# Three images' queries and the last context's high parts move into the end of the linear attention, and the high parts get two buffers

## Chip, cores and metric

The kernel runs on one core of one Trainium2 chip. The time is the device time of one launch in microseconds (us), the median of several runs. The profile is of one further execution.

## What is computed

The program is two layers of a network on x, 4 images of 512 tokens with 256 channels, each sublayer followed by a residual and a layer norm. Only layer 1's linear attention and its cross attention are touched by the change. The context `y` has 1601 tokens of 192 channels for each image.

```python
def _L1_attn_ref(H, W_qkv, b_qkv, W_proj, b_proj, gamma, beta):
    qkv = jnp.einsum('bnd,ed->bne', H, W_qkv) + b_qkv
    q, k, v = ...                            # 16 heads of 16
    q = _phi(q)                              # elu(x) + 1
    k = _phi(k)
    kv = jnp.einsum('bhnd,bhnv->bhdv', k, v)
    ...
    out = qkv_out / jnp.clip(qk1, 1e-06, None)
    out = out.reshape(B, N, D)
    out = jnp.einsum('bnd,ed->bne', out, W_proj) + b_proj
    out = (out - mu) * jax.lax.rsqrt(var + LN_EPS) * gamma + beta
    return out + residual

def _L1_xattn_ref(x, y, Wq, bq, Wk, bk, Wv, bv, Wo, bo):
    q = x @ Wq + bq
    k = y @ Wk + bk
    v = y @ Wv + bv
    ...                                      # 8 heads of 32
    weight = jnp.einsum('bhqd,bhkd->bhqk', q, k) * scale
    weight = jax.nn.softmax(weight, axis=-1)
    out = jnp.einsum('bhqk,bhkd->bhqd', weight, v)
    return out @ Wo + bo

x = _layernorm(x + _L1_attn_ref(x, ...), axis=-1)
x = _layernorm(x + _L1_xattn_ref(x, ctx_768, ...), axis=-1)
```

## The kernel before

The stages run one after the other, and a stage ends when all five engines have waited for its last results (`settle`). Within a stage each engine's program is written by walking one list of steps, the plan. An engine takes its instructions strictly in that order and waits on semaphores for what others deliver, so the plan sets the order of work on TensorE (PE), VectorE (DVE), ScalarE (ACT), GpSimd (POOL) and in SP's DMA queue alike.

**Linear attention** (`linear_plan`). For each image b: `inputs` (the projections to q, k and v), `state`, `read`, `regroup` (transposes, 16 stores to DRAM and one load back, `la_rg`), `project` (output projection, then a norm chain on DVE of evictions, statistics, scaling and the gamma multiply L2016, with the beta sum on POOL), `close` (residual L2020 and the second norm) and `channels` (transposes of the result into `x_ch`). With these, `mingle` spreads a side list evenly: work of the cross attention that doesn't depend on x, for images 0 to 2 (`AHEAD` is 3).

**The side list.** Matrix products of float32 data are made of bfloat16 parts, a high part and the rest (low). For the context of an image, `parts` is two casts on ACT (`xa_c_high` L2162 and `xa_c_both` L2163), and `context` is the subtraction of `xa_c_low` on DVE (L2134) and one on POOL in `xa_c_both` (L2178). `keys` (4 steps for an image, L2110, with ACT L2170 and DVE L2139 behind them) and `value` (7 steps, L2120, DVE L2145) read these parts. `keys`, and `value`, use the PSUM pairs of banks 0 and 2 in turn. There is one buffer of each part, so that `parts` of image b+1 waits for the last `value` of image b.

**Cross attention** (`cross_plan`). A prefix comes first: for each of the 4 images `x_split` (ACT casts `x_ch` into the high half of `xa_x_hl` L2554, POOL subtracts the low half L2623), two `queries` steps of 6 matmuls (L2369; ACT L2564 writes the high half, DVE L2474 the low half of `xa_q_hl`) and `asked` (SP stores it to DRAM, L2334); image 3's `parts`, `context`, `keys` and `value`; and 25 `maximum` steps (L2382, of 1024 or 577 columns; DVE reduces each, L2479). Then `pair` k is a matmul step of the scores of two heads (L2405) and an exponential on ACT (L2575), and `product` k multiplies the result into the sums (L2420). 208 pairs follow. Their rows are loaded from DRAM by units of two heads (`load`, L2323), the first three behind `asked` 0.

## Time and profile before

| | |
|---|---|
| time, median of 3 runs | 2854.57 us (2853.91 to 2859.57) |
| the profiled execution's own time | 2848.74 us |
| its span on the core | 2847.4 us |
| PE busy | 2229.3 us (78%) |
| DVE busy | 1674.0 us (59%) |
| ACT busy | 1182.0 us (42%) |
| mean granted clock of TensorE | 0.876 of full |
| linear attention | 1193.2 to 1398.2 us |
| prefix of the cross attention | 1398.2 to 1477.2 us |
| first to last pair | 1477.2 to 1932.6 us |

A timeline row gives start and duration in us, the engine, the line and the operation, what it wrote from what, how many, and in brackets the engine's idle time before it with what ended it. A busy PE is not PE at its peak: the same matmul takes about twice as long when the granted clock is low. "SPq" is SP's DMA issue, with the time of issue alone.

### The profile page before, as it was taken

What the parts mean: (1) busy time and instruction counts of PE and PEld (TensorE: products, weight loads), DVE (VectorE), ACT (ScalarE), POOL (GpSimd) and SP (SyncE); (2) the same over time, 40 slices, a digit from 0 to 9 for tenths busy, and PEclk for the clock granted to TensorE, in tenths of its full rate; (3) what the DMA queues carried; (4) which work ended last, traced back from release to release, by engine and by line L of the source; (5) the groups of instructions that cost most, each with busy time, mean ns of one, the idle gap of its engine ahead of it and who ended that gap; (6) DMA issues with size and microseconds to landing.
All of it is one profiled execution on the core that took longest, in us unless ns stands there. A gap on an engine that the chain in (4) does not pass through costs nothing. (4 is left out here: it accounts for less than half of the span.)

```text
span 2847.4 us, 41664 instructions
## 1 busy us (share of the span) xinstructions
PE 2229.3 (78%) x15694; PEld 1432.6 (50%) x15694; DVE 1674.0 (59%) x3413; ACT 1182.0 (42%) x2185; POOL 566.6 (20%) x489
## 2 busy tenths in 40 slices
PE   6993589896408999287589999995888697788678
PEld 3552157573306888144235555653555444455534
DVE  4666965568763333466556565643777642677663
ACT  2222844345232333132225555553665442566442
POOL 2110000001363554401200000001222141322052
PEclk9996789998658999589689999997899898899999
DMA  3005000100360111323311111102000001000000
GB/s 109 1 1 155 14 1 1 45 1 1 96 215 26 46 46 38 108 65 79 102 48 36 24 36 24 24 13 88 1 1 1 11 1 59 1 1 1 36 12 23
DMA packets 75074, 113.30 MB, mean 40 GB/s; under 512 B 22916, under 2 KB 59744, under 8 KB 74208
## 3 DMA queue, kind: packets, MB, share of 16 engines
q1 hardware_dynamic: 71808, 102.24, 12.0%
q0 software_dynamic: 3072, 8.39, 0.9%
q8 instruction: 131, 2.15, 0.3%
q14 instruction: 63, 0.52, 0.1%
HBM read 85.38 MB, written 31.20 MB: 41 GB/s over the span
## 5 line engine op out<-in xcount | busy, mean ns | idle before, releaser
L2479 DVE TENSOR_REDUCE xa_max<-psum 128x1 f32<-128x1024 f32 (+1 forms) x256 | 248.8, 988 | 144.7 <-PE psum L2382 144.1
L2575 ACT ACTIVATE xa_work<-psum 128x1024 f32<-128x1024 f32 (+1 forms) x208 | 212.9, 1024 | 202.1 <-PE psum L2405 200.5
L2420 PE MATMUL psum<-xa_work,xa_values 128*33 128x128 f32 (+1 forms) x3328 | 232.1, 284 | 0.0
L2420 PEld LDWEIGHTS psum<-xa_work,xa_values 128*33 128x33 f32 (+1 forms) x3328 | 172.9, 114 | 78.9 <-issue 73.7
L2774 PE MATMUL psum<-wqkv_l,x_hl_l 128*128 128x512 bf16 x576 | 146.1, 401 | 60.6 <-POOL x_hl_l L3034 32.4
L3140 PE MATMUL psum<-h_ch_f,w_f 128*128 128x512 bf16 (+1 forms) x576 | 139.3, 400 | 32.1 <-DVE h_ch_f L3200 9.5
L1645 DVE TENSOR_SCALAR moe_raw<-psum,tile_b 128x256 f32<-128x256 f32 x184 | 78.3, 474 | 139.3 <-PE psum L1487 138.2
L2405 PE MATMUL psum<-xa_query_rows,xa_key_rows 98*128 98x512 bf16 (+1 forms) x416 | 131.5, 399 | 8.4 <-ACT xa_work L2575 7.7
L1741 POOL TENSOR_TENSOR x_ch<-moe_raw,x_ch 128x512 bf16<-128x512 f32 x92 | 105.5, 1158 | 149.9 <-ACT x_ch L1701 147.8
L1487 PE MATMUL psum<-moe_rows,moe_w 128*128 128x256 bf16 x1104 | 132.9, 279 | 3.0 <-POOL moe_rows L1737 3.0
L2382 PE MATMUL psum<-xa_key_rows,xa_query_rows 96*128 96x512 bf16 (+1 forms) x512 | 129.4, 348 | 6.7 <-DVE xa_max L2479 3.0
L1498 PE MATMUL psum<-moe_w,x_ch 128*128 x1104 | 130.2, 280 | 0.0
L3008 ACT ACTIVATE w_p_l<-psum,w_max_l 128x256 f32<-128x256 f32 (+1 forms) x256 | 110.6, 458 | 28.8 <-DVE w_max_l L2912 28.6
L2774 PEld LDWEIGHTS psum<-wqkv_l,x_hl_l 128*128 128x128 bf16 x576 | 56.0, 102 | 130.3 <-issue 48.6
L1487 PEld LDWEIGHTS psum<-moe_rows,moe_w 128*128 x1104 | 110.0, 100 | 18.8 <-issue 4.2
L1498 PEld LDWEIGHTS psum<-moe_w,x_ch 128*128 128x128 bf16 x1104 | 110.9, 101 | 16.7 <-issue 1.3
L3140 PEld LDWEIGHTS psum<-h_ch_f,w_f 128*128 128x128 bf16 (+1 forms) x576 | 56.8, 102 | 111.4 <-issue 33.9
L1038 PE MATMUL psum<-ctx_f,query_sum 128*128 128x512 f32 (+1 forms) x256 | 105.5, 538 | 7.9 <-DVE query_sum L1090 7.9
L3045 POOL TENSOR_TENSOR qk_other_l<-qk_raw_l,rotary_l 128x256 f32<-128x256 f32 x64 | 64.7, 1011 | 196.0 <-DVE qk_rot_l L2896 196.0
L1059 PE MATMUL psum<-ctx_f,probs_t_bn 128*128 128x128 f32 (+1 forms) x832 | 100.0, 277 | 2.8 <-DVE probs_t_bn L1116 2.8
L1701 ACT CAST x_ch<-moe_raw 128x512 bf16<-128x512 f32 x92 | 56.9, 618 | 101.4 <-DVE moe_raw L1645 101.4
L1174 POOL TENSOR_TENSOR x_tok<-x_tok,rows 128x4096 f32<-128x4096 f32 x1 | 8.8, 8809 | 451.5 <-DVE fused L1135 451.5
(439 smaller groups left out, 4832.2 us busy)
## 6 DMA issues: line engine op xcount, KB each, us to landing
xa_key_rows<-cross_keys SPq DMA_DIRECT2D x48, 200.1 KB, 3.5
moe_raw<-in_moe_w SPq DMA_DIRECT2D x16, 512.0 KB, 5.2
x_ch<-in_moe_w SPq DMA_DIRECT2D x16, 512.0 KB, 4.8
moe_rows<-slots_in SPq DMA_DIRECT2D x23, 256.0 KB, 2.8
slots_out<-moe_rows SPq DMA_DIRECT2D x23, 256.0 KB, 2.1
ctx_f<-in_ctxT SPq DMA_DIRECT2D x2, 2401.5 KB, 21.5
cross_keys<-xa_k_hl SPq DMA_DIRECT2D x6, 800.5 KB, 3.7
xa_query_rows<-cross_queries SPq DMA_DIRECT2D x48, 64.0 KB, 3.5
```

Source lines behind the costliest of these rows:

```text
L1038: ins = pe.matmul(u.wide[:, c0 - a:c1 - a], t["qsum"][:, n * P:(n + 1) * P], t["keys"][:, b * S2 + c0:b * S2 + c1], start=True, stop=True)
L1487: ins = pe.matmul(u.ap[:, a * SLOT:(a + 1) * SLOT], w1[:, w, h, cf], t["x"][j % 2][:, x, h, :], start=(h, k) == (0, 0), stop=(h, k) == (1, 2))
L1498: ins = pe.matmul(u.ap[:, a * D:(a + 1) * D], t["hidden"][j % 2][:, x, f, q], w2[:, w, f, :], start=(f, k) == (0, 0), stop=(f, k) == (7, 2))
L1741: g.tensor_tensor(hidden[:, 1, f, :], t["act"][n % 2], hidden[:, 0, f, :], ALU.subtract).then_inc(*s.h_low.up())
L2382: ins = pe.matmul(u.wide[:, x - c0:y - c0], t["q_rows"][n % 3][0:SPLIT, a, qt * P:(qt + 1) * P], t["k_rows"][n % 3][0:SPLIT, a, x:y], star ...
L2405: ins = pe.matmul(u.wide[0:rows, a * T:(a + 1) * T], t["k_rows"][n % 3][:, a, kt * P:kt * P + rows], t["q_rows"][n % 3][:, a, :], start=Tr ...
L2420: ins = pe.matmul(total.ap[a * LANE:a * LANE + VC, c:c + PIECE], t["v"][b][0:rows, kt, first + a, :], exps[0:rows, a, c:c + PIECE], start= ...
L2479: v.tensor_reduce(t["maxes"][n % 2][:, qt * HU + a, part:part + 1], u.wide[:, 0:c1 - c0], AX.X, ALU.max).then_inc(*u.free)
L2575: act.activation(t["exps"][k % EXPS][0:rows], u.wide[0:rows].rearrange("p (m q) -> p m q", q=T), ACT.Exp, scale=1.0 / float(np.sqrt(np.flo ...
L2774: ins = pe.matmul(b.ap, x[:, i, h, w * P:(w + 1) * P], t["wqkv"][:, j, h, cols], start=(h, n) == (0, 0), stop=(h, n) == (1, 2))
L3008: ins = act.activation(t["p"][n % 2][:, i, lo:2 * P], scores[:, i, :], ACT.Exp, bias=t["peak"][n % 2][:, i:i + 1], scale=8.0, accum_out=t[ ...
L3140: ins = pe.matmul(u.ap[0:rows, :], t["w1"][:, y, h, o:o + rows], t["h_ch"][g % 2][:, x, h, :], start=(h, n) == (0, 0), stop=(h, n) == (1, 2))
```

## The change

- `linear_plan` is written in pieces, each still placed whole (its "coarse order"), and the pieces of a `project` or `close` step get names of their own (`spread`, `root`, `scale`; `close`, `root_last`, `finish`).
- At its end stand `x_split`, `queries` and `asked` of images 0, 1 and 2, with one buffer each of `q_hl` and `x_hl`. The weights `xa_q` are loaded and split with those of keys and values.
- `xa_c_high` and `xa_c_both` have two buffers, `xa_c_low` and `xa_ctx_f` one. `parts` of image b+1 stands between the values of image b; `context` (the low part) stays behind the last of them. `parts` and `context` of image 3 are the last of the side list.
- `cross_plan` starts with the keys of image 3, and its prefix has only image 3's `x_split`, `queries` and `asked`, which end it. SP issues the rows of the first three units at the stage's start. The exponentials wait for the store of image 3's queries, as their buffers lie in the same memory.
- `la_oc` has one buffer instead of two. In `kv` steps ACT makes the exponential before the copy.

```diff
+    inputs = lambda b: [[("q", b, c) for c in range(HALVES)] + [("kv", b, n) for n in range(TPB)]]
...
+    close = lambda b: [[("close", b), ("root_last", b), ("finish", b)]]
+    regroup, channels, split = lambda b: [[("regroup", b)]], lambda b: [[("channels", b)]], lambda b: [[("x_split", b)]]
+    queries = lambda b: [[("queries", b, c) for c in range(HALVES)] + [("asked", b)]]
...
-    plan += [("channels", B - 3), ("close", B - 2), ("project", B - 1), ("close", B - 1), ("channels", B - 2), ("channels", B - 1)]
-    side = [("weights",)] + flat([[("parts", b), ("context", b)] + key_steps(b) + value_steps(b) for b in range(AHEAD)])
-    return plan[:2] + mingle(plan[2:], side)
+    pieces += channels(B - 3) + split(0) + close(B - 2) + queries(0) + split(1) + project(B - 1) + queries(1) + close(B - 1)
+    pieces += channels(B - 2) + split(2) + channels(B - 1) + queries(2)
+    side = [[("weights",)]]
+    for b in range(AHEAD):
+        values = value_steps(b)
+        steps = ([("parts", b)] if b == 0 else []) + [("context", b)] + key_steps(b) + values[:4] + [("parts", b + 1)] + values[4:]
+        side += [[step] for step in steps]
+    side.append([("context", AHEAD)])
+    return flat(pieces[:2] + mingle(pieces[2:], side))
...
-        settle(m, [use["channels", B - 1, h].done for h in range(HALVES)] + [use["value", AHEAD - 1, KT - 1].done]
-               + [s.k_stored0.now(), s.k_stored1.now(), s.v_ones.now()])
+               + [s.q_stored.now(), s.a_low.now(), s.b_low.now(), s.k_stored0.now(), s.k_stored1.now(), s.v_ones.now()])
...
     elif kind == "context":
-        n = step[1] - first
-        v.wait_ge(*s.c_split(2 * n + 1))
-        v.tensor_tensor(t["c_low"][:, 0:S2], t["ctx_f"][:, 0, :], t["c_high"][:, 0:S2], ALU.subtract).then_inc(*s.a_low.up())
+        b, = step[1:]
+        v.wait_ge(*s.c_split(2 * b + 1))
+        if b:
+            v.wait_ge(*use["value", b - 1, KT - 1].full)
+        v.tensor_tensor(t["c_low"][:, 0:S2], t["ctx_f"][:, 0, :], t["c_high"][b % 2][:, 0:S2], ALU.subtract).then_inc(*s.a_low.up())
...
+    elif kind == "x_split":
+        b, = step[1:]
+        if b > first:
+            for c in range(HALVES):
+                act.wait_ge(*use["queries", b - 1, c].full)
...
+        act.copy(t["x_hl"][:, 0], m.x_ch[:, :, b * T:(b + 1) * T]).then_inc(*s.x_high.up())
...
-        if n:
-            act.wait_ge(*use["value", b - 1, KT - 1].full)
-        act.copy(t["c_high"][:, 0:S2], t["ctx_f"][:, 0, :]).then_inc(*s.c_split.up())
+        if b > 1:
+            act.wait_ge(*use["value", b - 2, KT - 1].full)
+        act.copy(t["c_high"][b % 2][:, 0:S2], t["ctx_f"][:, 0, :]).then_inc(*s.c_split.up())
...
-    rest = asked(2) + asked(3) + flat([key_steps(b) + value_steps(b) for b in range(AHEAD, B)])
-    plan = asked(0) + [("parts", B - 1), ("context", B - 1)] + asked(1) + mingle(rest, maxima[:lead])
+    rest = key_steps(AHEAD) + [("x_split", AHEAD)] + value_steps(AHEAD) + [("queries", AHEAD, c) for c in range(HALVES)] + [("asked", AHEAD)]
+    plan = rest[:2] + mingle(maxima[:lead], rest[2:])
...
+                act.wait_ge(*s.q_stored(16))
```

Three places show the order. First PE, where the linear attention ends and the cross attention begins; before the change the last values (`xa_wv`) are followed by the queries (`xa_wq`) of images 0 and 1, and those of 2 and 3 alternate with maxima:

```order
L2120 MATMUL psum<-xa_wv,xa_c_high 65x256
L2120 MATMUL psum<-xa_wv,xa_c_low 65x256
L2120 MATMUL psum<-xa_wv,xa_c_high 65x256
L2120 MATMUL psum<-xa_wv,xa_c_both 65x256 x2
L2369 MATMUL psum<-xa_x_hl,xa_wq 128x512 x24
L2382 MATMUL psum<-xa_key_rows,xa_query_rows 128x512 x2
L2369 MATMUL psum<-xa_x_hl,xa_wq 128x512 x6
L2382 MATMUL psum<-xa_key_rows,xa_query_rows 128x512
L2382 MATMUL psum<-xa_key_rows,xa_query_rows 128x65
```

After the change image 2's queries stand ahead of the last value step, which ends the linear attention:

```order
L2142 MATMUL psum<-xa_x_hl_l,xa_wq 128x512 x12
L2167 MATMUL psum<-xa_wv,xa_c_high 65x256
L2167 MATMUL psum<-xa_wv,xa_c_low 65x256
L2167 MATMUL psum<-xa_wv,xa_c_high 65x256
L2167 MATMUL psum<-xa_wv,xa_c_both 65x256 x2
```

and the cross attention's first maxima stand right behind its first keys (`xa_wk`):

```order
L2157 MATMUL psum<-xa_c_both,xa_wk 128x512 x2
L2157 MATMUL psum<-xa_c_high,xa_wk 128x65
L2157 MATMUL psum<-xa_c_low,xa_wk 128x65
L2157 MATMUL psum<-xa_c_high,xa_wk 128x65
L2157 MATMUL psum<-xa_c_both,xa_wk 128x65 x2
L2420 MATMUL psum<-xa_key_rows,xa_query_rows 128x512 x3
L2420 MATMUL psum<-xa_key_rows,xa_query_rows 128x65
```

So 36 of the 48 query matmuls have left the prefix, and 12 of these stand just ahead of the linear attention's end.

Second DVE in the linear attention, at image 1's low part of the context (`xa_c_low`). Before, it stands ahead of image 1's norm chain:

```order
L2134 TENSOR_TENSOR xa_c_low<-xa_ctx_f,xa_c_high 128x1601
L2139 SCALAR_TENSOR_TENSOR xa_k_hl<-psum,cols,xa_k_hl 128x1024
L2003 TENSOR_TENSOR x_ch<-psum,rows 128x256 x4
L2006 BN_STATS ln_stats<-x_ch 128x6 x4
L2009 BN_AGGR ln_mean_var<-ln_stats 128x2 x4
L2011 RECIPROCAL ln_rstd<-ln_std 128x4
L2014 TENSOR_SCALAR x_ch<-x_ch,ln_mean_var,ln_rstd 128x256 x4
L2016 TENSOR_TENSOR x_ch<-x_ch,rows 128x2x512
```

After the change, behind it and behind the last value eviction of image 0, with the first keys of image 1 behind it:

```order
L2015 TENSOR_TENSOR x_ch<-psum,rows 128x256 x4
L2040 BN_STATS ln_stats<-x_ch 128x6 x4
L2044 BN_AGGR ln_mean_var<-ln_stats 128x2 x4
L2051 RECIPROCAL ln_rstd<-ln_std 128x4
L2054 TENSOR_SCALAR x_ch<-x_ch,ln_mean_var,ln_rstd 128x256 x4
L2023 TENSOR_TENSOR x_ch<-x_ch,rows 128x2x512
L2199 TENSOR_TENSOR xa_values<-psum,rows 65x8x32
L2188 TENSOR_TENSOR xa_c_low<-xa_ctx_f,xa_c_high 128x1601
L2193 SCALAR_TENSOR_TENSOR xa_k_hl<-psum,cols,xa_k_hl 128x1024
```

So the keys of image 1 now wait for a subtraction that stands behind the norm chain.

Third ACT near the linear attention's end. Before, the casts of image 2's context (`xa_c_high`, `xa_c_both`) stand two rows ahead of its keys (`xa_k_hl`):

```order
L1298 COPY x_ch<-psum 128x512
L2162 CAST xa_c_high<-xa_ctx_f 128x1601
L2163 CAST xa_c_both<-xa_ctx_f 128x1601
L225 ACTIVATE ln_std<-ln_mean_var,eps 128x4
L2170 ACTIVATE xa_k_hl<-psum,cols 128x1024
L2170 ACTIVATE xa_k_hl<-psum,cols 128x577
```

After the change the same casts are further ahead of the keys, with two rows of other work more between them; a cast of `x_ch` for the queries and the two query evictions are new:

```order
L1298 COPY x_ch<-psum 128x512
L2093 ACTIVATE ln_std<-ln_mean_var,eps 128x4
L2232 CAST xa_c_high<-xa_ctx_f 128x1601
L2233 CAST xa_c_both<-xa_ctx_f 128x1601
L1298 COPY x_ch<-psum 128x512
L2219 CAST xa_x_hl_l<-x_ch 128x1024
L2093 ACTIVATE ln_std<-ln_mean_var,eps 128x4
L2240 ACTIVATE xa_k_hl<-psum,cols 128x1024
L2226 ACTIVATE xa_q_hl_l<-psum,cols 128x512 x2
L2240 ACTIVATE xa_k_hl<-psum,cols 128x577
```

So the casts of a context no longer stand at the place where its keys are due, and ACT has the queries' work there.

## Rows read from the trace of the kernel before

**Rows 1.** Busy time by stretch; columns as the first line names them.
```profile
core 0: us, PE busy (x) PEld busy (x) DVE busy (x) ACT busy (x) POOL busy (x), PEclk, DMA share, GB/s
...
1355.00:1398.00 43.00, 32.64 (x145) 16.73 (x145) 29.27 (x74) 6.33 (x11) 2.35 (x1) 0.72 0.15 51
1398.00:1420.00 22.00, 7.79 (x20) 2.70 (x21) 4.23 (x6) 7.22 (x8) 10.83 (x5) 0.62 0.75 192
1420.00:1446.00 26.00, 15.92 (x48) 5.45 (x47) 11.17 (x14) 5.59 (x8) 10.50 (x7) 0.67 0.31 76
1446.00:1477.00 31.00, 27.04 (x141) 10.83 (x140) 23.33 (x32) 3.72 (x4) 0.00 (x0) 0.94 0.19 70
1480.00:1600.00 120.00, 119.14 (x1210) 69.76 (x1210) 75.84 (x106) 64.19 (x69) 2.35 (x1) 0.97 0.12 29
```

**Rows 2.** Timeline of all engines, the first images of queries.
```profile
start us, us, engine line op out<-in xcount [idle before <-releaser]
...
1398.22 1.04 ACT L2554 CAST xa_x_hl<-x_ch 128x1024 bf16<-128x1024 f32 x1 [3.91 <-DVE xa_values L2145]
...
1399.44 2.12 POOL L2623 TENSOR_TENSOR xa_x_hl<-x_ch,xa_x_hl 128x1024 bf16<-128x1024 f32 x1 [17.75 <-ACT xa_x_hl L2554]
...
1402.81 4.63 PE L2369 MATMUL psum<-xa_x_hl,xa_wq 128*128 128x512 bf16 x12 [5.20 <-DVE xa_wq L2464]
...
1405.57 0.69 ACT L2564 ACTIVATE xa_q_hl<-psum,cols 128x512 bf16<-128x512 f32 x1 [3.94 <-PE psum L2369]
...
1406.29 0.75 DVE L2474 SCALAR_TENSOR_TENSOR xa_q_hl<-psum,cols,xa_q_hl 128x512 bf16<-128x512 f32 x1 [3.70 <-ACT xa_q_hl L2564]
...
1409.03 0.37 SPq L2334 DMA_DIRECT2D cross_queries<-xa_q_hl  x1
...
1412.00 0.33 SPq L2323 DMA_DIRECT2D xa_key_rows<-cross_keys  x1
...
1416.84 4.45 PE L2369 MATMUL psum<-xa_x_hl,xa_wq 128*128 128x512 bf16 x12 [9.40 <-issue]
```

**Rows 3.** Timeline of TensorE until the first pair.
```profile
1421.13 0.60 PE L2382 MATMUL psum<-xa_key_rows,xa_query_rows 96*128 96x512 bf16 x2
1428.67 2.72 PE L2369 MATMUL psum<-xa_x_hl,xa_wq 128*128 128x512 bf16 x6 [6.95 <-issue]
...
1446.66 2.63 PE L2110 MATMUL psum<-xa_work,xa_wk 128*128 128x512 bf16 x10 [0.33 <-DVE xa_max L2479]
...
1454.34 4.24 PE L2110 MATMUL psum<-xa_work,xa_wk 128*128 128x512 bf16 x10 [0.24 <-DVE xa_max L2479]
...
1477.20 0.60 PE L2405 MATMUL psum<-xa_query_rows,xa_key_rows 98*128 98x512 bf16 x2
```

**Rows 4.** Timeline of VectorE, maxima one behind the other.
```profile
1435.69 3.67 DVE L2479 TENSOR_REDUCE xa_max<-psum 128x1 f32<-128x1024 f32 x4
```

**Rows 5.** Timeline of TensorE, last 43 us of the linear attention.
```profile
1355.10 0.58 PE L2110 MATMUL psum<-xa_c_high,xa_wk 128*128 128x512 bf16 x1 [6.83 <-POOL xa_c_both L2178]
...
1379.85 0.39 PE L2120 MATMUL psum<-xa_wv,xa_c_high 128*128 128x256 bf16 x1 [5.29 <-DVE xa_values L2145]
...
1387.42 0.39 PE L2120 MATMUL psum<-xa_wv,xa_c_high 128*128 128x256 bf16 x1 [3.01 <-DVE xa_values L2145]
...
1397.12 0.50 PE L2120 MATMUL psum<-xa_wv,xa_c_both 128*65 128x256 bf16 x2
```

**Rows 6.** Timeline of VectorE, the same stage from 1300 us on.
```profile
1303.53 1.82 DVE L2134 TENSOR_TENSOR xa_c_low<-xa_ctx_f,xa_c_high 128x1601 bf16<-128x1601 f32 x1
...
1314.35 0.42 DVE L2003 TENSOR_TENSOR x_ch<-psum,rows 128x256 f32<-128x256 f32 x1 [0.44 <-PE psum L1926]
...
1318.49 1.23 DVE L2016 TENSOR_TENSOR x_ch<-x_ch,rows 128x1024 f32<-128x1024 f32 x1
...
1351.67 4.25 DVE L2020 SCALAR_TENSOR_TENSOR x_tok<-x_tok,x_ch 128x1024 f32<-128x1024 f32 x1
...
1367.16 1.22 DVE L2020 SCALAR_TENSOR_TENSOR x_tok<-x_tok,x_ch 128x1024 f32<-128x1024 f32 x1
```

**Rows 7.** Timeline of GpSimd there.
```profile
1351.46 3.39 POOL L2178 TENSOR_TENSOR xa_c_both<-xa_ctx_f,xa_c_both 64x1601 bf16<-64x1601 f32 x1 [3.27 <-ACT xa_c_both L2163]
```

**Rows 8.** Timeline of TensorE at image 1's context.
```profile
1305.45 0.58 PE L2110 MATMUL psum<-xa_c_high,xa_wk 128*128 128x512 bf16 x1 [2.89 <-DVE xa_c_low L2134]
```

More of the change, by code:

```diff
@@ L1794, in linear_attention @@
         plan = linear_plan()
-        norms = [p for p in plan if p[0] in ("project", "close")]
-        nth = {p: n + 1 for n, p in enumerate(norms)}
+        nth = {p: n + 1 for n, p in enumerate(p for p in plan if p[0] in ("root", "root_last"))}
         steps = []
         for step in plan:
-            kind, b = step[0], step[-1]
-            if kind == "inputs":
-                steps += [("q", b, c) for c in range(2)] + [("kv", b, n) for n in range(TPB)]
-            elif kind == "state":
-                steps.append(("state", b))
-            elif kind in ("read", "project"):
-                steps += [(kind, b, n) for n in range(TPB)]
-            elif kind in ("regroup", "channels"):
-                steps += [(kind, b, h) for h in range(HALVES)]
+            if step[0] in ("q", "kv", "state", "read", "project"):
+                steps.append(step)
+            elif step[0] in ("regroup", "channels"):
+                steps += [step + (h,) for h in range(HALVES)]
@@ L1808, in linear_attention @@
         use = m.banks(steps, (4, 5, 6, 7))
-        use.update(m.banks([p for p in plan if p[0] in ("keys", "value")], (0, 2)))
+        use.update(m.banks([p for p in plan if p[0] in ("keys", "value", "queries")], (0, 2)))
         linear_sp(m, s, t, use, plan)
@@ L1903, in linear_pe @@
         elif kind == "read":
+            n, u = step[2], use[step]
             pe.wait_ge(*use["state", b].done)
-            for n in range(TPB):
-                u = use["read", b, n]
-                pe.wait_ge(*u.empty)
-                for h in range(HALVES):
-                    ins = pe.matmul(u.ap[:, h * CV:(h + 1) * CV], t["q"][b % 2][:, h, n * P:(n + 1) * P], t["kvd"][b % 2][:, h, :],
-                                    start=True, stop=True)
-                ins.then_inc(*u.fill)
+            pe.wait_ge(*u.empty)
+            for h in range(HALVES):
+                ins = pe.matmul(u.ap[:, h * CV:(h + 1) * CV], t["q"][b % 2][:, h, n * P:(n + 1) * P], t["kvd"][b % 2][:, h, :],
+                                start=True, stop=True)
+            ins.then_inc(*u.fill)
         elif kind == "regroup":
@@ L2097, in prepare_pe @@
     pe, kind = m.nc.tensor, step[0]
-    if kind == "keys":
+    if kind == "queries":
+        b, c = step[1:]
+        u = use[step]
+        pe.wait_ge(*s.x_low(b - first + 1))
+        pe.wait_ge(*u.empty)
+        for h in range(HALVES):
+            for n, (x, w) in enumerate(PASSES):
+                ins = pe.matmul(u.ap, t["wq"][:, w, h, c * P:(c + 1) * P], t["x_hl"][:, x, h, :],
+                                start=(h, n) == (0, 0), stop=(h, n) == (1, 2))
+        ins.then_inc(*u.fill)
+    elif kind == "keys":
         b, o, c0 = step[1:]
@@ L2202, in cross_plan @@
 def cross_plan():
-    def asked(b):
-        return [("x_split", b)] + [("queries", b, c) for c in range(HALVES)] + [("asked", b)]
     maxima = []
@@ L2299, in rows_loaded @@
     return (s.rows0, s.rows1, s.rows2)[u % 3]
-def asked_stored(s, b):
-    return (s.q_stored0, s.q_stored1)[b % 2]
 def max_loaded(s, u):
@@ L2360, in cross_pe @@
         kind = step[0]
-        if kind == "queries":
-            b, c = step[1:]
-            u = use[step]
-            pe.wait_ge(*s.w_low(1))
-            pe.wait_ge(*s.x_low(b + 1))
-            pe.wait_ge(*u.empty)
-            for h in range(HALVES):
-                for n, (x, w) in enumerate(PASSES):
-                    ins = pe.matmul(u.ap, t["wq"][:, w, h, c * P:(c + 1) * P], t["x_hl"][b % 2][:, x, h, :],
-                                    start=(h, n) == (0, 0), stop=(h, n) == (1, 2))
-            ins.then_inc(*u.fill)
-        elif kind in PREPARED:
+        if kind in PREPARED:
             prepare_pe(m, s, t, use, step, AHEAD)
```

416 lines of the change are left out of this document (206 added, 210 removed).

## Prediction

> **What bounds the kernel now.** I first read the busy time by stretch [rows 1]. From the first pair of the cross attention on, TensorE is the bound: 119.14 of 120 us busy. Nothing of the change touches that part, so it moves only in as far as it starts earlier. Ahead of it lie two stretches in which no engine is full. The prefix of the cross attention lasts from 1398.2 to 1477.2 us, 79.0 us: in its first 22 us TensorE is busy for 7.79 us at a granted clock of 0.62, in the next 26 for 15.92 at 0.67, and only the last 31 are dense (27.04 us, clock 0.94). The last 43 us of the linear attention have 32.64 us of TensorE and 29.27 of VectorE, at a clock of 0.72.
>
> Then the timeline of the prefix. Image 0's queries are a chain: ScalarE's cast at 1398.22, GpSimd's subtraction (2.12 us), the weights' split, 12 matmuls in 4.63 us, evictions of 0.69 and 0.75 us, the store issued at 1409.03, and only at 1412.00 the first load of rows [rows 2]. TensorE waits 5.20 us, then 9.40 for image 1's split, which stands behind image 3's context on ScalarE and GpSimd [rows 2], then 6.95 for image 2's, which stands behind the memory fills of GpSimd [rows 3]. The keys of image 3 begin at 1446.66, the first pair at 1477.20 [rows 3]. So 48.5 of the 79.0 us pass before the dense part.
>
> **The prefix after the change.** All of its inputs are there when it begins. I build it from the piece that was dense before:
> - 1446.66 to 1477.20 held all keys and values of image 3 and 15 of the 25 maxima before the first pair (counted in the plan): 30.5 us.
> - The other 10 maxima come into it. Four in a row took VectorE 3.67 us [rows 4], 0.92 each: 9.2 us. VectorE was idle 31.0 - 23.33 = 7.7 us in that stretch [rows 1], but mostly behind ScalarE's key evictions, so I deduct nothing.
> - Two query steps of image 3: 6 matmuls take 2.3 to 2.7 us at the low clock and half of that at the full one, and an eviction of 0.75 on VectorE behind 0.69 on ScalarE [rows 2, 3]: 2.6 us together.
> - The start. The first keys run at the low clock: 4.24 us for 10 matmuls against 2.63 [rows 3], so about 1.6 more. The first maximum needs unit 0's rows. Before, its load was issued at 1412.00 and the maximum ran at 1421.13, behind other work, so they need at most 9.1 us [rows 2, 3]; keys fill some 7 of them. Together 3.3 us.
> - A new wait: the exponentials may not write until image 3's queries are stored. From the store's issue to the load that waited for it passed 2.97 us [rows 2]. TensorE, with three PSUM pairs, stands still nearly as long: 3.0 us.
>
> Sum 30.5 + 9.2 + 2.6 + 3.3 + 3.0 = 48.6 us in place of 79.0: **30.4 us less**. Bounds: if the added work fills VectorE's 7.7 idle us, 41 (38 less); if the low clock lasts through all keys and values (estimate: 8 us more, as 1.6 for each of four groups of 10 key matmuls and as much again for half the values), 57 (22 less).
>
> **The linear attention after the change.**
> - Queries of images 0 to 2: 36 matmuls. One image took 4.63 us at the low clock [rows 2]. Image 0's come where the clock was high (estimate: half, 2.3), the others where it was low: 2.3 + 4.6 + 4.6 = 11.5 us. Images 1 and 2 stand beside TensorE's two longest waits there, 5.29 and 3.01 us for VectorE's norm chains [rows 5]. They share their PSUM pairs with keys and values, and the second step needs a pair that VectorE still holds; I take 5 of the 8.3 us as cover. Cost +6.5. With no cover and all at the low clock 13.9, with full cover 3.2.
> - VectorE gets 6 evictions of 0.75 and image 3's low part of 1.82, 6.3 us; ScalarE 3 casts of 1.04, 6 evictions of 0.69 (7.3 us) [rows 2, 6] and the casts of image 3's context. In the last 43 us they were idle for 13.7 and 36.7 [rows 1]. Nothing, as long as they don't lie ahead of a norm.
> - Image 2's context. TensorE waited 6.83 us for casts and GpSimd's 3.39 us [rows 5, 7]. Both now come during image 1's values. What is left is the last value eviction (0.4, as the eviction of 256 columns at 1314.35) and the low part (1.82) [rows 6]: 2.3. Gain -4.5.
> - Image 1's context. The wait was 2.89 us [rows 8]. The low part now stands behind image 1's norm chain, which from its last eviction at 1314.35 to the end of the gamma multiply takes 5.4 us [rows 6]; with 0.4 and 1.82 behind it that is 7.6 us, of which TensorE fills about 1.9 (estimate) with the last values and the transposes. Wait 5.7, cost +2.8. Behind the waiting keys stand state 3 and read 3, with image 3's whole chain; I count that delay once, since that chain has slack until its projection. If ScalarE and VectorE come through sooner, 0; at worst twice, 5.6.
> - The stage's end. Before, it closed 0.6 us after the last matmul (1397.6 [rows 5] to 1398.2). Now image 2's queries end one step before the last value: 0.69 + 0.75 + a store of 3.0, that is 4.4 us behind them, 3.5 behind the last matmul. Cost +3.0.
> - The second `la_oc` buffer is gone: its stores lie tens of us apart, so nothing. The order of exponential and copy: nothing either way beyond 1 us.
>
> Sum 6.5 - 4.5 + 2.8 + 3.0 = **7.8 us more**. By the ends above: about 0 to 20.
>
> **Port.** VectorE's residual (L2020) took 4.25 us at 1351.67, beside GpSimd's subtraction of 1351.46 to 1354.85, and 1.22 us alone [rows 6, 7]: 3.03 us of standstill. The change puts three GpSimd subtractions of 2.12 us and one of 3.39 more into the stage. I count none on the path, since two of them follow a `channels` step and few instructions with two SBUF inputs stand there; the bound is one standstill for each of three, 9.1 us. The Trainium skill's page "SBUF — State Buffer", section "SBUF: two separate sides", says that these two engines share a port pair as an exclusive lock when VectorE's instruction has two SBUF inputs and GpSimd's reads SBUF, and the later one is fully blocked. The trace agrees, with the 3.03 us above. Taken as certain at each of the three splits it would make the sum 9.1 us worse, which is a rival below.
>
> **The time.** -30.4 + 7.8 = -22.6 us. From the profiled execution's 2848.74 us that gives 2826.1. The runs' median, 2854.57, lies 5.8 above it: 2832 us.
>
> **The rivals.**
> - *The prefix gets still better* (chance 0.10). The stage is dense from the start, and the dense stretches had a clock of 0.94 to 0.97 against 0.62 and 0.67 [rows 1]. With 38 less there and 3 more in the linear attention: -35, 2820 us. Against it: the 25 maxima alone are 23 us of VectorE (25 x 0.92), and each step of the keys passes three engines in turn.
> - *The port* (0.07): each of the three splits blocks a norm or residual of VectorE on the path, +9.1: 2841 us. For it the 3.03 us of rows 6 and 7; against it that an instruction must stand ready just as GpSimd begins: one that comes later waits only for what is left.
> - *Only the work moves* (0.10). The prefix was bound by something that stays (loads, keys), and saves only its query matmuls, 3 x 4.6 = 13.9 us, while the linear attention grows by 7.8: -6.1, 2848 us, half of this case below the bound of 0.2%. For it: 24 query matmuls and the loads overlap in 1412 to 1421. Against it: waits of 9.40 and 6.95 us for splits alone.
> - *The queries don't overlap at the new place* (0.06), the case of a slower kernel. Each image's chain from cast to store lies on the path, as it did from 1398.22 to 1409.03 [rows 2], 10.8 us; 3 x 10.8 + 3.0 at the end = 35.4, against 30.4 saved: +5.0, and 2860 us. It decides once the linear attention grows by more than 30 us. Against it: between one image's split and its queries stand several steps of keys and values, and the split's inputs are ready early.
>
> **How the numbers follow.** The forecast has 0.67, the others as given. Its own range is 2822 to 2843. A measurement of this kernel can tell about 0.2%, 5.7 us, from no change. The range for 8 in 10 reaches from the better prefix, 2820, less a little, to the port case with some of the third: 2818 to 2846. Faster: 0.67 + 0.10 + 0.07 + half of 0.10 = 0.89, put at 0.88; same 0.06; slower 0.06.
>
> **What would show it.** In the profile after: the first pair 46 to 52 us after the linear attention's end; no wait above 4 us of TensorE there, save one for ScalarE at the first pairs; the granted clock above 0.85 in most of the prefix. The linear attention closes 213 us after its first instruction in place of 205 (1193.2 to 1398.2), with a wait of 5 to 6 us for `xa_c_low` at image 1, about 2.3 at image 2, and some 4 us without matmuls at its end. I am wrong if the linear attention grows by over 20 us, if the rows' loads hold the first maxima beyond 10 us, or if the stretch of the pairs, which I take as unchanged at some 455 us, changes its clock.

## The result, and the profile after

The changed kernel takes 2813.34 us (median of 4 runs, 2811.14 to 2816.53) against 2855.36 us (4 runs, 2853.91 to 2859.57): ratio 0.9851, 95% interval 0.9834 to 0.9868. It is faster, by 42 us where 23 were forecast, and lies below the range of 2818 to 2846. The profiled execution took 2813.72 us with a span of 2812.4, which is 35.0 us less than the span before.

Where the 35 us lie, by stage (each from the first or last instruction of the stage in the two traces; the last pair by the start of its last matmul, so the stretch of the pairs is 455.7 us before where the table ahead of the prediction gives 455.4):

| stretch | before, us | after, us | difference | forecast |
|---|---|---|---|---|
| until the linear attention | 1193.2 | 1198.1 | +4.9 | 0 |
| linear attention | 205.0 | 216.4 | +11.4 | +7.8 |
| its end to the first exponential | 81.0 | 49.4 | -31.6 | -30.4 |
| first exponential to the last pair | 453.7 | 438.6 | -15.1 | 0 |
| behind the last pair | 914.5 | 909.9 | -4.6 | 0 |

The first and the last stretch are the same program in both kernels. In the 20 profiles of this case the first matmul of the linear attention stands at 1195.3 to 1206.3 us and the stretch behind the last pair takes 909.2 to 915.0, with the kernel before and the changed one on both sides of each other, so +4.9 and -4.6 are the spread of executions and no effect of the change.

The prefix of the cross attention by stretch of time in the changed kernel, then the same 120 us of pairs as in [rows 1] and the end of the linear attention, with the columns of [rows 1]:

```profile
1414.50:1436.00 21.50, 15.82 (x64) 5.03 (x66) 13.33 (x16) 4.64 (x5) 3.29 (x2) 0.90 0.80 202
1436.00:1458.40 22.40, 20.58 (x107) 8.96 (x107) 18.43 (x26) 1.06 (x2) 8.28 (x6) 0.87 0.00 1
1371.00:1414.50 43.50, 32.89 (x165) 16.18 (x165) 27.96 (x57) 13.99 (x18) 9.85 (x4) 0.93 0.29 96
1480.00:1600.00 120.00, 119.69 (x1231) 71.79 (x1232) 76.55 (x109) 64.20 (x68) 2.35 (x1) 1.00 0.11 29
```

In place of 22 us with 7.79 us of TensorE at a clock of 0.62 [rows 1] the stage starts with 15.82 of 21.5 us at 0.90, and the first pair comes 43.8 us behind the start. The waits that the prediction named stand in TensorE's timeline:

```profile
1318.15 0.63 PE L2157 MATMUL psum<-xa_c_low,xa_wk 128*128 128x512 bf16 x1 [6.49 <-issue]
1368.14 0.63 PE L2157 MATMUL psum<-xa_c_low,xa_wk 128*128 128x512 bf16 x1 [3.83 <-DVE xa_c_low L2188]
1372.45 1.96 PE L2142 MATMUL psum<-xa_x_hl_l,xa_wq 128*128 128x512 bf16 x6
1375.20 1.45 PE L2142 MATMUL psum<-xa_x_hl_l,xa_wq 128*128 128x512 bf16 x6 [0.79 <-DVE xa_k_hl L2193]
1385.99 1.47 PE L2142 MATMUL psum<-xa_x_hl_l,xa_wq 128*128 128x512 bf16 x6
1391.02 2.72 PE L2142 MATMUL psum<-xa_x_hl_l,xa_wq 128*128 128x512 bf16 x6 [3.56 <-DVE xa_k_hl L2193]
1414.64 0.58 PE L2157 MATMUL psum<-xa_c_high,xa_wk 128*128 128x512 bf16 x1 [3.32 <-DMA cross_queries<-xa_q_hl_l]
1420.53 0.60 PE L2420 MATMUL psum<-xa_key_rows,xa_query_rows 96*128 96x512 bf16 x2
1458.32 0.59 PE L2443 MATMUL psum<-xa_query_rows,xa_key_rows 98*128 98x512 bf16 x2
1465.00 1.04 PE L2420 MATMUL psum<-xa_key_rows,xa_query_rows 96*128 96x512 bf16 x2 [3.71 <-ACT xa_work L2591]
```

The first row is image 1's context, the second image 2's, then two rows each for the queries of images 0 and 1, the wait for the last store of queries at the stage's end, the first maximum (5.9 us behind the start), the first pair, and the standstill of TensorE while ScalarE's exponentials wait for image 3's store.

Ahead of image 2's keys stands what the prediction counted as not on the path: GpSimd's split of image 0, and beside it VectorE's low part of image 2's context, which takes 2.97 us here and 1.82 in [rows 6].

```profile
1363.85 2.12 POOL L2250 TENSOR_TENSOR xa_x_hl_l<-x_ch,xa_x_hl_l 128x1024 bf16<-128x1024 f32 x1
1364.68 2.97 DVE L2188 TENSOR_TENSOR xa_c_low<-xa_ctx_f,xa_c_high 128x1601 bf16<-128x1601 f32 x1
```

What no step of the prediction has is the stretch of the pairs. Its program is the same in both kernels, yet from the first to the last pair it takes 455.7 us before and 444.2 after. The place where they part is the first image's end. First the kernel before, busy time of TensorE and granted clock by 3 us:

```profile
core 0: us, PE busy (x), PEclk, DMA share, GB/s
1611.00:1614.00 3.00, 3.00 (x38) 1.00 0.03 7
1614.00:1617.00 3.00, 2.25 (x24) 1.00 0.43 99
1617.00:1620.00 3.00, 1.20 (x3) 0.71 0.75 172
1620.00:1623.00 3.00, 3.00 (x21) 0.50 0.00 0
1623.00:1626.00 3.00, 3.00 (x20) 0.50 0.00 0
1626.00:1629.00 3.00, 3.00 (x16) 0.50 0.00 0
1629.00:1632.00 3.00, 3.00 (x22) 0.51 0.00 0
1632.00:1635.00 3.00, 3.00 (x35) 1.00 0.02 5
```

and the changed kernel at the same place of the program:

```profile
1599.00:1602.00 3.00, 1.83 (x21) 1.00 0.51 128
1602.00:1605.00 3.00, 1.61 (x20) 1.00 0.55 145
1605.00:1608.00 3.00, 3.00 (x30) 1.00 0.00 0
1608.00:1611.00 3.00, 2.28 (x22) 1.00 0.03 5
1611.00:1614.00 3.00, 3.00 (x32) 1.00 0.00 0
```

The wait ahead of both is the same to the hundredth: TensorE stands still for ScalarE's load of the exponential's table behind the layer norm's square root. The row of TensorE before:

```profile
1618.80 1.01 PE L2405 MATMUL psum<-xa_query_rows,xa_key_rows 98*128 98x512 bf16 x2 [2.56 <-ACT xa_work L2575]
```

and after:

```profile
1603.39 0.59 PE L2443 MATMUL psum<-xa_query_rows,xa_key_rows 98*128 98x512 bf16 x2 [2.56 <-ACT xa_work L2591]
```

The same two matmuls then take 1.01 us at the clock of 0.50 (1.2 GHz) before and 0.59 at 1.00 (2.4 GHz) after. What the low clock costs is read from ScalarE's table loads at two ends in a row. Before:

```profile
1616.34 1.28 ACT L2575 ACT_TABLE_LOAD   x1
...
1735.73 1.28 ACT L2575 ACT_TABLE_LOAD   x1
```

After:

```profile
1600.93 1.28 ACT L2591 ACT_TABLE_LOAD   x1
...
1715.17 1.28 ACT L2591 ACT_TABLE_LOAD   x1
```

119.39 us against 114.24: the second interval, whose end had no low clock, is 5.15 us shorter, so some 14 us at the low clock cost 5.15 us.

### The profile page after: what moved, and what is told of

Same layout as the page of the kernel before. It is cut to its first block and busy times, and to the rows that moved or that the text cites. A ratio compares the mean times of both kernels' runs of the same rounds, so it can differ in the third digit from the quotient of the medians.

```text
span 2812.4 us, 41641 instructions
## 1 busy us (share of the span) xinstructions
PE 2188.7 (78%) x15624; PEld 1422.1 (51%) x15694; DVE 1672.9 (59%) x3413; ACT 1179.7 (42%) x2185; POOL 567.4 (20%) x489
## 5 line engine op out<-in xcount | busy, mean ns | idle before, releaser
L2458 PE MATMUL psum<-xa_work,xa_values 128*33 128x128 f32 (+1 forms) x3328 | 223.9, 277 | 0.0
L2781 PE MATMUL psum<-wqkv_l,x_hl_l 128*128 128x512 bf16 x538 | 136.9, 400 | 65.7 <-POOL x_hl_l L3041 32.9
```

Of the source, the lines that this page charges most:

```text
L2458: ins = pe.matmul(total.ap[a * LANE:a * LANE + VC, c:c + PIECE], t["v"][b][0:rows, kt, first + a, :], exps[0:rows, a, c:c + PIECE], start= ...
L2781: ins = pe.matmul(b.ap, x[:, i, h, w * P:(w + 1) * P], t["wqkv"][:, j, h, cols], start=(h, n) == (0, 0), stop=(h, n) == (1, 2))
```

## The experiments

**Moving the pairs in time.** Theory *place in time*: whether the granted clock falls behind one and the same standstill depends on when the standstill comes. Rival *layout*: something in the changed kernel's memory or order does it. The first edit lets all engines stand still at the start of the cross attention, for n memory fills of 0.91 us on VectorE, 1.2 us each with the signals around them; it was made in the changed kernel (after_pause) and in the one before (before_pause).

```diff
+def pause(m, tile, times):
+    nc, s = m.nc, m.signals("paused", first=80)
+    for n in range(times):
+        nc.vector.memset(tile, 0.0).then_inc(*s.paused.up())
+        nc.vector.wait_ge(*s.paused.now())
+    for e in (nc.tensor, nc.scalar, nc.gpsimd, nc.sync):
+        e.wait_ge(*s.paused.now())
...
+        pause(m, t["o_ch"], 2)
         cross_sp(m, s, t, use, plan)
```

> The changed kernel, with a standstill of all engines at the start of the cross attention, made of two memory fills of 128x1024 on VectorE one behind the other (estimate: 1 to 2.5 us in all); nothing else is altered. Theory 'phase': the time of the pairs differs between the two kernels because the granted clock answers to the same 2.56 us standstill at an image's end in one kernel and not in the other, by where in time the standstill falls. Then the stretch from the first to the last pair, 444 us in the changed kernel and 456 before, moves by steps of about 5 us when the whole stretch is shifted, and the total changes by something else than the pause: -10 to +12 us. Theory 'layout': where the tiles lie in memory makes the difference. Then the stretch stays at 444 us and the total grows by the pause alone, 1 to 2.5 us.

> As the run with two fills, but with four (estimate: 2 to 5 us in all). Phase: the stretch of the pairs need not be 444 us nor what it is with two fills; at least one of the two differs from 444 by 4 us or more. Layout: 444 us, and 2 to 5 us more in total.

> The kernel before, with the same standstill of two fills at the start of its cross attention. Phase: its stretch of the pairs leaves 456 us by 4 us or more in this run or in the one with four fills, most likely downwards, since two of its three image ends already had the low clock; then the total falls although the kernel only stands still longer. Layout: 456 us, and 1 to 2.5 us more in total.

> The kernel before, with four fills. Phase: as for two. Layout: 456 us, and 2 to 5 us more in total.

> The changed kernel as it is, once more. If its 2813 us belong to the place in time at which its standstills fall, and that place is nearly the same in every execution, 2811 to 2818 us and a stretch of the pairs near 444 us; if the place is a matter of chance in each execution, values up to about 2830 us appear among its runs, as one of the 22 of the kernel before came out at 2830.64 against a median of 2852.74.

> The changed kernel with a standstill of one fill (0.91 us of VectorE and the signals around it, about 1.2 us) at the start of the cross attention. Phase: between 2814 and 2840 us, as two fills gave 2825 and four 2841, and the stretch of the pairs is at 444 or at 457 us, not between because of the pause. Rival, that only the length of the standstill counts: the time grows in order with the number of fills, so here 2816 to 2820 us.

> With three fills (about 3.6 us). Rival, length alone: between the times of two and four fills, 2825 to 2841 us. Phase: it may lie outside of these, and the time less the pause differs from the neighbours' by steps of 5 us or more.

> The kernel before with one fill. Phase: 2845 to 2860 us, its stretch of the pairs near 456 us as in the kernel itself and with two and four fills, or at 444 us and then some 10 us less. With this run the mean over five kernels each (none, one, two, three, four fills; four for the kernel before), each less its pause, gives what the change is worth apart from the luck of the clock: by the sum of the prediction -22.6 us, by the two medians alone -42 us.

The second edit holds TensorE alone, once, in the middle of image 0's pairs, until GpSimd has filled a tile of 128x64 that nothing else uses n times (held). The tile is new, so the tiles behind it in memory move by its size; it is the same in both held forms.

```diff
+HELD = 30
...
+            if k == HELD:
+                pe.wait_ge(*m.held(2))
...
+        elif step == ("pair", HELD - 1):
+            g.wait_ge(*s.multiplied(HELD - BEHIND + 1))
+            for n in range(2):
+                g.memset(t["fill"][:], 0.0).then_inc(*m.held.up())
+                g.wait_ge(*m.held.now())
```

> The kernel before, with TensorE held once in the middle of image 0's pairs, until GpSimd has filled a small unused tile twice (estimate: 0.8 to 1.3 us of standstill). Place in time decides: the three ends of images come later by the standstill, and at least the first is followed by something else than the 14 us of low clock that it had in all four profiles, most likely none or 3 us; the stretch of the pairs is 5 to 12 us shorter than 455.7 although the kernel stands still once more. Layout: 14 us of low clock at each of the three ends as before, and 456.5 to 457 us.

> The same with four fills (estimate: 1.5 to 2.4 us of standstill). Place in time: the pattern at the ends is another one than in the kernel before and than with two fills. Layout: 14 us of low clock at each end, 457 to 458 us.

> The changed kernel, held in the same way with two fills. Place in time: the first end of an image, which had no low clock in any of the profiles with a stretch of 444 to 448 us, may have it now; the stretch is 444 plus the standstill plus 0, 5 or 12 us. Layout: 445 to 446 us.

> The same with four fills. Place in time: in this run or in the one with two fills the stretch is over 449 us, with low clock after the first end. Layout: 446 to 447 us in both.

All of them, and the changed kernel in two more measurements (the second, after_paired, is told below). "Low clock" is worked out from windows of 1 us in the profiled execution, each with its mean clock c, as the sum of (1 - c)/0.5: behind the start of the pairs, and behind the ends of images 0, 1 and 2. "Pairs" is the profiled stretch from the start of the first to that of the last matmul of the pairs. The last column is the median of the kernel before, measured together with that row.

| kernel | pairs, us | low clock, us | median (lowest to highest), us | before |
|---|---|---|---|---|
| before | 455.7 | 7, 14, 14, 14 | 2855.4 (2853.9 to 2859.6) | |
| before_pause1 | 455.7 | 7, 14, 14, 14 | 2844.7 (2831.8 to 2854.5) | 2848.7 |
| before_pause2 | 455.7 | 7, 14, 14, 14 | 2851.7 (2848.1 to 2862.0) | 2852.7 |
| before_pause4 | 455.3 | 7, 14, 14, 14 | 2855.1 (2839.0 to 2859.2) | 2852.7 |
| before_held2 | 441.4 | 7, 0, 3, 0 | 2825.9 (2824.9 to 2833.2) | 2841.9 |
| before_held4 | 445.6 | 7, 0, 3, 10 | 2832.2 (2831.1 to 2837.2) | 2841.9 |
| after | 444.2 | 10, 0, 3, 0 | 2813.3 (2811.1 to 2816.5) | 2855.4 |
| after_again | 447.9 | 10, 0, 3, 10 | 2811.1 (2806.8 to 2818.7) | 2848.7 |
| after_paired | 444.2 | 10, 0, 3, 0 | 2803.4 (2799.9 to 2810.0) | 2840.3 |
| after_pause1 | 444.2 | 10, 0, 3, 0 | 2818.2 (2812.4 to 2821.0) | 2848.7 |
| after_pause2 | 457.3 | 10, 10, 14, 14 | 2825.0 (2820.3 to 2842.1) | 2852.7 |
| after_pause3 | 447.9 | 10, 0, 3, 10 | 2821.0 (2816.8 to 2823.6) | 2848.7 |
| after_pause4 | 456.8 | 7, 10, 14, 14 | 2841.4 (2826.6 to 2842.2) | 2852.7 |
| after_held2 | 445.5 | 10, 0, 3, 3 | 2806.2 (2800.6 to 2808.2) | 2841.9 |
| after_held4 | 458.5 | 10, 10, 14, 14 | 2807.1 (2800.0 to 2820.0) | 2841.9 |

With two and four fills the changed kernel's pairs are at 457 us; with none, one and three they are at 444 to 448. That speaks against the rival that only the length of the standstill counts for the pairs, and against the layout, which is the same in all of them; each is one profile, though, and the medians do grow nearly in order with the fills. The pauses changed the prefix too: in after_pause4 it took 54.1 us from the stage's first matmul to the first pair, against 43.7 to 47.2 with three fills or fewer. The kernel before stayed at 455.3 to 455.7 with every pause, against the expectation, so its side was open until it was held in the middle.

The expectation of before_pause1 asks for the mean difference of the two kernels with the same number of fills. Three fills were run in the changed kernel alone; for the others the medians in the table give 37.6 us (after_again), 26.4 (one fill), 26.8 (two) and 13.7 (four), 26.1 in the mean, against 22.6 forecast by the sum.

In before_held2 TensorE stood still for half a microsecond more, by its row:

```profile
1534.41 0.60 PE L2408 MATMUL psum<-xa_query_rows,xa_key_rows 98*128 98x512 bf16 x2 [0.49 <-POOL xa_fill L2644]
```

and at the end of image 0 the clock no longer falls (windows of 3 us), though the standstill there is as long as ever (TensorE's timeline):

```profile
1608.00:1611.00 3.00, 2.29 (x24) 1.00 0.40 103
1611.00:1614.00 3.00, 1.15 (x12) 1.00 0.66 168
1614.00:1617.00 3.00, 3.00 (x36) 1.00 0.01 3
```

```profile
1612.86 0.59 PE L2408 MATMUL psum<-xa_query_rows,xa_key_rows 98*128 98x512 bf16 x2 [2.57 <-ACT xa_work L2578]
```

Half a microsecond more of standing still took 14.3 us off the pairs and 16.0 us off the median (2825.87 against 2841.90; ratio 0.9954, interval 0.9939 to 0.9969), and every one of its five executions is shorter than every one of the ten of the kernel before beside it. What TensorE does ahead of that end is the same in both kernels and with the hold: in the 18 us ahead of that standstill it has one gap of 0.26 us, some 6 us ahead of the second table load, and no other of over 0.05 us. So its work there isn't what differs. The other way round, 0.91 us in the changed kernel (after_held4) brought the low clock to an end of an image that had none; its hold, and the windows at that end:

```profile
1518.55 0.61 PE L2446 MATMUL psum<-xa_query_rows,xa_key_rows 98*128 98x512 bf16 x2 [0.91 <-POOL xa_fill L2651]
```

```profile
1595.00:1598.00 3.00, 1.01 (x8) 1.00 0.78 180
1598.00:1601.00 3.00, 3.00 (x20) 0.54 0.00 0
1601.00:1604.00 3.00, 3.00 (x20) 0.50 0.00 0
1604.00:1607.00 3.00, 3.00 (x20) 0.50 0.02 5
1607.00:1610.00 3.00, 3.00 (x27) 0.76 0.00 0
```

Layout cannot be the reason there: after_held2 and after_held4 have the same tiles in the same places and 445.5 and 458.5 us. Nor can it be for the third end, which had no low clock in after and 10 us in after_again, the same kernel. On the side of the kernel before the new tile came with the hold, and no run has the tile without it.

The profiled execution of after_held4 is also the longest of its four, 2820.0 us against a median of 2807.1. One kernel can fall on one side or the other from execution to execution: after and after_again show it, and the wide spreads of others (after_pause4, before_pause1) suggest it. Of 68 timed executions of the kernel before, too, two took 2830.6 and 2822.4 us, some 20 below their medians, at mean granted clocks of 0.884 and 0.887 where the rest of their series have 0.873 to 0.881.

The traces also show what the place is relative to. In 18 of the 20 profiles (all but both and both_paired) the clock is low for a while behind the first pair and then rises. From that rise to the second table load at the end of image 0 it is 127.8 to 128.0 us in the four profiles of the kernel before without a hold, and 14 us of low clock follow; 128.1 to 129.0 us in eleven others, and none follows; 129.1 to 129.4 us in after_pause2, after_pause4 and after_held4, and 10 us follow. The three groups do not overlap. So the pauses never moved the pairs of the kernel before against the clock's own changes (127.8, 127.8 and 128.0 against 127.8 without one), and the hold, which lies behind the rise, did (128.4). That fits its pauses changing nothing there.

The Trainium skill's page "TensorE: Matmul & The Clock Gate", section "Part 1: The HAM clock gate (the "warmup" mystery)", says that the window in which the gate watches activity is free-running and does not start anew with a kernel. The runs agree in so far as the pairs of the kernel before took 441.4 us with a standstill of 0.49 us more, and 455.7 without it; the window itself no run shows.

**The parts ahead.** The edit casts each image's high parts again right ahead of its own low part; the two buffers stay.

```diff
-        steps = ([("parts", b)] if b == 0 else []) + [("context", b)] + key_steps(b) + values[:4] + [("parts", b + 1)] + values[4:]
+        steps = [("parts", b), ("context", b)] + key_steps(b) + values
...
-    side.append([("context", AHEAD)])
+    side += [[("parts", AHEAD)], [("context", AHEAD)]]
```

> The changed kernel without one of its parts: each image's high parts are cast again right ahead of its own low part, not during the values of the image before; the two buffers stay. By the prediction's terms image 2's wait for its context grows from the 3.83 us measured after the change by 4.5 us (the term is judged by the wait itself), image 1's, where VectorE's norm chain comes last, shrinks or stays; the linear attention lasts 2 to 6 us longer than 216.4 us. Rival: the chain of VectorE hides the casts at both places, and the stage stays within 1 us. The total is not the judge, since the clock in the pairs may move it by 13 us on its own.

Median 2818.50 us (2814.66 to 2828.28), the kernel before at 2844.61. From the first matmul of the linear attention to that of the cross attention it took 217.4 us. The changed kernel took 210.5, 207.8, 208.4, 208.1, 208.1 and 207.6 in the six profiles that do the same up to there (after, after_again, after_paired, the two held ones, own_room), the kernel before 199.5 (up to ScalarE's cast, its first instruction there), and 200.0 and 199.4 in its held forms. TensorE's waits for image 1's and image 2's parts:

```profile
1315.48 0.59 PE L2157 MATMUL psum<-xa_c_high,xa_wk 128*128 128x512 bf16 x1 [12.27 <-POOL xa_c_both L2258]
...
1364.67 0.59 PE L2157 MATMUL psum<-xa_c_high,xa_wk 128*128 128x512 bf16 x1 [6.75 <-POOL xa_c_both L2258]
```

Image 2's wait is 2.9 us longer than the 3.83 us with the parts ahead, less than the 4.5 expected, image 1's 5.8 us longer than 6.49 where it was expected not to grow. Casting ahead is worth 6.9 to 9.8 us, and most of it at image 1, where the prediction had put a loss.

**The first exponentials.** The last image's queries get memory that the exponentials do not write (the place of an output tile that is used 100 us later):

```diff
-        q_room, x_room = (work[:, n:n + HALVES * T].bitcast(BF16).rearrange("p (x h q) -> p x h q", x=2, h=HALVES)
-                          for n in (2 * S2, 2 * S2 + HALVES * T))
+        q_room, x_room = (room.bitcast(BF16).rearrange("p (x h q) -> p x h q", x=2, h=HALVES)
+                          for room in (spare[:, TPB * D:2 * TPB * D], work[:, 2 * S2 + HALVES * T:2 * S2 + 2 * HALVES * T]))
...
+            if b == 1 and first == 0:
+                v.wait_ge(*s.q_stored(16))
...
-                act.wait_ge(*s.q_stored(16))
+                act.wait_ge(*use["queries", AHEAD, 1].full)
```

> The changed kernel with the last image's queries in memory that the exponentials do not write (the place of an output tile that is used 100 us later), so that the first exponentials do not wait for the store. The wait of TensorE for ScalarE at the first pairs, 3.71 us, goes: 3 to 4 us less from the linear attention's end to the fourth pair. Rival: the load of ScalarE's table (1.28 us) or the maxima's chain stands right behind it, and less than 1 us is gained. The total by the clock: 2806 to 2830 us.

Median 2801.43 us (2799.02 to 2803.78), the kernel before at 2844.61, ratio 0.9842 (0.9826 to 0.9859). ScalarE's table load in the changed kernel, and behind it the same in own_room:

```profile
1462.62 1.28 ACT L2591 ACT_TABLE_LOAD   x1 [3.91 <-DMA cross_queries<-xa_work]
1463.92 1.94 ACT L2591 ACTIVATE xa_work<-psum 128x1024 f32<-128x1024 f32 x2
```

```profile
1450.68 1.28 ACT L2593 ACT_TABLE_LOAD   x1 [0.31 <-PE psum L2443]
1451.98 2.12 ACT L2593 ACTIVATE xa_work<-psum 128x1024 f32<-128x1024 f32 x2
```

The wait falls from 3.91 to 0.31 us, and from the stage's start to the first exponential pass 45.8 us in place of 49.3. From there to the last pair it is 438.6 us in both kernels, so nothing of the 3.5 us is given back.

**The low part ahead of the norm chain.** Image 0's last value step and image 1's low part stand ahead of image 1's projection on every engine:

```diff
+    moved = [("value", 0, KT - 1), ("context", 1)]
+    plan = [step for step in plan if step not in moved]
+    at = plan.index(("project", 1, 0))
+    return plan[:at] + moved + plan[at:]
```

> The changed kernel with image 0's last value step and image 1's low part put ahead of image 1's projection on every engine, so that the low part does not stand behind the norm chain. The wait of 6.49 us for the low part at image 1 falls to 2 to 3 us; image 1's norm starts some 2 us later. The linear attention is 1 to 4 us shorter than 216.4 us. Rival: the delay of the norm chain comes back at image 1's close and later steps, and the stage stays within 1 us.

Median 2805.84 us (2799.21 to 2817.98), the kernel before at 2844.61, ratio 0.9875 (0.9844 to 0.9905). The stage takes 200.3 us on the measure above, 7 to 10 us less than the changed kernel's 207.6 to 210.5, about twice what was expected at most. The keys of image 1 no longer wait:

```profile
1304.48 1.04 PE L1938 MATMUL psum<-const,la_o 128*128 128x128 f32 x8
1305.36 0.38 PE L2161 MATMUL psum<-xa_c_high,xa_wk 128*128 128x512 bf16 x1
1305.57 0.38 PE L2161 MATMUL psum<-xa_c_low,xa_wk 128*128 128x512 bf16 x1
```

The whole wait of 6.49 us is gone, and the matmuls of 512 columns that took 0.63 us behind it run in 0.38. The delay of the norm chain did not come back within the stage.

**Both edits,** and both beside the changed kernel on one chip:

> Both of these edits in one: their effects add, 4 to 8 us less up to the fourth pair than in the changed kernel; the total by the clock of the pairs 2803 to 2826 us.

> The changed kernel as it is, beside the version with both edits on the same chip. 2800 to 2818 us by the chip; ratio to the kernel before 0.985 to 0.987, as in its two measurements.

> The version with both edits. If the waits that it takes out are worth their length, it is 6 to 14 us below the changed kernel beside it; if the clock takes them back, within 4 us of it.

Both: 2797.11 us (2794.95 to 2800.70), ratio 0.9827 (0.9811 to 0.9844). In the profile, from the first matmul of the linear attention to the start of the cross attention 201.3 us and from there to the first exponential 47.2, together 248.5 (the same in both_paired), against 257.7 (208.4 + 49.3) in after_paired; no low clock at the start of the pairs, 3, 0 and 3 us at the ends, 438.5 us of pairs. Side by side: changed kernel 2803.44 us (2799.87 to 2810.03), ratio 0.9865 (0.9851 to 0.9879); both edits 2795.96 us (2788.37 to 2812.05), ratio 0.9854 (0.9826 to 0.9881). The medians are 7.5 us apart, as expected, but the intervals overlap: four of its six executions lie below all four of the changed kernel, and two (2810.2 and 2812.1 us, at clocks of 0.882 and 0.881 where the four have 0.888 to 0.892) above them. It is the best version by the median in both measurements, and in the profile by its waits; that it is faster in the mean is not clear of noise.

## Why the prediction was wrong

- **The prefix, -30.4 us: right.** To the first exponential it fell by 31.6. The sum of 48.6 us ended behind the store wait, at the first exponential, and is measured there with 49.4; the 79.0 it was set against ended at the first pair, 2.0 us earlier, so on one footing the forecast was 32.4. It starts from one profile: the prefix up to the first pair, 79.0 us there, took 74.1 to 79.0 in the five other profiles of the kernel before, and 43.7 to 47.2 in the changed one's without a pause. The first maximum came 5.9 us behind the start, the store wait was 3.7 where 3.0 were put.
- **The linear attention, +7.8 us: nearly right.** +11.4 in the profile shown. On the measure of the experiments it is 11.0 in this one and 8.1 to 8.9 in the five others that do the same up to there. The waits are 6.49 us at image 1 (5.7 forecast), 3.83 at image 2 (2.3) and 3.32 at the end (3.0). The queries met waits of 0.79 and 3.56 us for a PSUM pair, as the prediction feared for the second step. One term was left out: the parts ahead shorten image 1's wait as well. Without them it is 12.27 us, and with the low part ahead of the norm chain there is none.
- **Port: one meeting of three was on the path.** The prediction counted none. Image 0's split on GpSimd made VectorE's low part of image 2's context last 2.97 us in place of 1.82, and TensorE waited for it: 1.15 of the 1.5 us by which that wait exceeds the forecast. It is 2.9 to 3.4 us in each of the profiles that have this order. The other two splits met no instruction of VectorE that took longer beside them.
- **Rivals.** The sum of both stages in this profile is -20.2 us against -22.6; no rival's time was met, the nearest (the better prefix, 2820 us) for a reason that it did not name.
- **The step that failed: "the stretch of the pairs, which I take as unchanged at some 455 us"**, and "it moves only in as far as it starts earlier". It was 11.5 us shorter, 444.2, and 15.1 shorter when counted from the first exponential, which leaves the store wait at its start out. The prediction read the clock of 0.97 in that stretch [rows 1] as a property of it. What the runs showed in its place: three standstills of 2.56 us, each followed by low clock for 0 to 14 us by where in time it falls, 5.15 us of time for 14 us of low clock. Before the change all of them were at the dear end in four profiles out of four; in six of the nine of the changed kernel, its paused and its held forms they had 3 to 14 us of low clock together in place of 41. The move of the start by some 19 us did what half a microsecond did in before_held2. Nothing in the change aims at it, so this part of the gain is luck, and a small edit ahead of the pairs can take it back, as after_pause2 shows. Where both kernels have the cheap places, in before_held2 and after_held2 beside each other, they are 2825.9 and 2806.2 us, 19.6 apart, close to the 22.6 that the sum gave.
- **What stays open.** In the two later measurements, both on one chip, the changed kernel was 37.6 us (2848.74 - 2811.10) and 36.9 us (2840.31 - 2803.44) below the kernel before, in the first 42.0. The profiles of before and after account for 20.2 us up to the first exponential and 15.1 behind it, 35.3. From the first matmul of the linear attention to the last pair the difference is 35.8 us by after, 31.3 by after_again and 37.8 by after_paired, so the profiles of one kernel differ by as much as is missing in the later measurements. The rest of the first 42.0 may lie in the profiled execution of the kernel before, which took 2848.74 us, 6.6 below the median of the four timed ones; no run told that apart. Why the edges between 14, 0 and 10 us of low clock lie at 128.0 and 129.0 us behind the rise is not shown either, and at the other two ends of images the places were not sorted out.

## What to carry to other kernels

Before a dense stretch is taken as unchanged, look for standstills of TensorE of a few microseconds in it and at the clock behind each: if a like one elsewhere has another clock behind it, the stretch can move by some per mille when anything ahead of it moves, and the range must hold that. Judge an edit by the waits and the stage times in the trace, and the total only with several shifts of the same kernel. Put a cast that needs nothing late ahead of where it is due (6.9 to 9.8 us here), and a small step that TensorE waits for ahead of a norm chain, not behind it (7 to 10 us here). When a GpSimd step is moved, look at each step of VectorE that will run beside it: one of three meetings cost 1.15 us of TensorE's wait here.

## What the runs showed of the hardware

- A standstill of TensorE of 0.49 us added in the middle of a dense stretch made the kernel 16.0 us faster; in its profile three later standstills of 2.56 us were followed by 3 us of low clock in all, not 41.
- Behind standstills of the same length the granted clock stood at 0.50 for 0, 3, 10 or 14 us; 14 us cost 5.15 us. At the end of image 0 it was 14, 0 or 10 us as the table load came 127.8 to 128.0, 128.1 to 129.0 or 129.1 to 129.4 us behind the clock's last rise.
- VectorE's low part (two inputs in SBUF) took 2.97 us in place of 1.82 beside a GpSimd subtraction.
- The kernel before has medians of 2840.3, 2841.9, 2844.6, 2848.7, 2852.7 and 2855.4 us in six measurements, a spread of 0.5%, and 2848.7 and 2840.3 are from one chip; the ratio of the changed kernel to it held to 0.9851, 0.9866 and 0.9865.
